# Attention with routed experts: the row maxima 22 slots ahead from the first unit to the last, a unit's shift turned behind step 22

## What is computed

```python
# x: [4, 1024, 128]; 16 heads of 8 dimensions
q, k, v = split(layernorm(layernorm(x)) @ w_qkv + b_qkv)
scores = q @ k.T * 8 ** -0.5 + rel_bias[h, i - j]
attn = softmax(scores) @ v
x = x + layernorm(attn @ w_out + b_out)
# 64 experts: a token takes 8 of them, out of its 4 best groups of 8
topk_idx, topk_w = route(layernorm(x) @ gate.T)
x = x + layernorm(experts(layernorm(x), topk_idx, topk_w) + shared(layernorm(x)))
```

## Time and profile before

| | before |
|---|---|
| median of 3 runs | 1193.54 us (1192.19 to 1193.61) |
| profiled execution, its own time | 1190.53 us |
| its span in the trace | 1188.6 us |
| mean granted TensorE clock | 0.87 of full |
| busy: PE, DVE, ACT, POOL | 883.5, 789.2, 689.8, 592.6 us |
| first step of unit 0, of unit 31 | 113.06 us, 867.30 us |
| PE idle ahead of `turn_shift` (L1328) for POOL | 8.3 us in 12 of 32 |

### The profile page before, as it was taken

How to read it: one execution, slowest core, us unless ns; L and a number is a source line. 1 busy time by engine, 2 the same in 40 slices (tenths; PEclk the granted TensorE clock), 3 DMA queues, 4 the chain that set the end, 5 groups by cost and what they waited for, 6 DMA issues and landing times. The chain is left out here.

```text
span 1188.6 us, 16268 instructions
## 1 busy us (share of the span) xinstructions
PE 883.5 (74%) x5090; PEld 274.5 (23%) x5090; DVE 789.2 (66%) x1222; ACT 689.8 (58%) x1433; POOL 592.6 (50%) x734
## 2 busy tenths in 40 slices
PE   4653999999889999989999998999973530555400
PEld 2410222222222222222222222222211320444300
DVE  7864888889869989968988987998711320111107
ACT  4721767787767777768778776777771210322204
POOL 5820010114255555635745644555575756478747
PEclk9865999999989999999999999999996675655655
DMA  3859523012211122220001120000000010767546
GB/s 99 242 157 133 113 65 103 20 37 65 71 54 27 30 56 73 67 46 7 8 14 36 39 69 15 5 5 16 6 5 22 19 46 3 182 130 135 99 96 208
DMA packets 110379, 77.97 MB, mean 66 GB/s; under 512 B 35359, under 2 KB 95259, under 8 KB 110294
## 3 DMA queue, kind: packets, MB, share of 16 engines
q1 hardware_dynamic: 87062, 68.21, 21.9%
q0 software_dynamic: 21504, 6.79, 4.8%
q10 hardware_dynamic: 1728, 1.94, 1.0%
HBM read 38.75 MB, written 54.95 MB: 79 GB/s over the span
## 5 line engine op out<-in xcount | busy, mean ns | idle before, releaser
L209 DVE TENSOR_REDUCE half_max<-s_pair 128x2 f32<-128x1024 f32 x512 | 601.9, 1217 | 113.1 <-PE s_pair L198 109.5
L1248 ACT ACTIVATE probs<-st_bank 128x512 f32<-128x512 f32 x1024 | 543.8, 603 | 171.6 <-PE st_bank L1308 171.2
L1111 POOL DMA_INDIRECT table<-rows,keys_i x256 | 256.7, 1003 | 179.4 <-issue 68.3
L1308 PE MATMUL st_bank<-q_stack,k_stack 98*128 98x512 bf16 (+1 forms) x1024 | 326.1, 390 | 10.1 <-ACT probs L1248 7.6
L1317 PE MATMUL pv_bank<-probs,values 128*9 128x512 f32 x2048 | 270.4, 600 | 3.1 <-ACT unit_out L1182 3.0
L198 PE MATMUL s_pair<-k_stack,q_stack 64*128 64x512 bf16 x1024 | 204.0, 398 | 41.4 <-DVE half_max L209 22.0
L198 PEld LDWEIGHTS s_pair<-k_stack,q_stack 64*128 64x128 bf16 x1024 | 49.4, 93 | 359.6 <-issue 185.2
L1491 POOL DMA_INDIRECT sums<-out,ids x64 | 99.7, 1558 | 40.7 <-ACT out L1546 18.4
L1308 PEld LDWEIGHTS st_bank<-q_stack,k_stack 98*128 98x128 bf16 (+1 forms) x1024 | 78.2, 97 | 170.1 <-issue 75.8
L1505 DVE CAST ids<-xe 128x4 uint32<-128x4 f32 x16 | 2.9, 180 | 136.2 <-DMA sums<-out,ids 84.5
L1005 POOL CAST shift<-minus_max 128x16 bf16<-128x16 f32 x32 | 6.4, 201 | 111.7 <-DVE minus_max L215 111.6
(11 more groups left out here) (181 smaller groups left out, 788.4 us busy)
## 6 DMA issues: line engine op xcount, KB each, us to landing
table<-blank SPq DMA_DIRECT2D x8, 772.0 KB, 7.4
xe<-table SPq DMA_DIRECT2D x16, 386.0 KB, 4.8
q_stack<-q_image SPq DMA_DIRECT2D x96, 64.0 KB
k_stack<-k_image SPq DMA_DIRECT2D x96, 64.0 KB
s<-sums SPq DMA_DIRECT2D x24, 256.0 KB, 6.0
k_image<-k_piece SPq DMA_DIRECT2D x16, 256.0 KB, 3.3
table<-rows,keys_i POOLq DMA_INDIRECT x256
sums<-zeros SPq DMA_DIRECT2D x16, 256.0 KB
```

The costliest lines, as they stand in the source:

```text
L209: nc.vector.tensor_reduce(halves[:, h:HG:SIDE_HEADS, tile, half], stacks.s_pair[slot % S_SLOTS][:].rearrange("p (s k) -> p s k", s=SIDES), ...
L1111: pool.indirect_dma_start(out=table, out_offset=bass.IndirectOffsetOnAxis(ap=keys_i[c % 2][:, pick:pick + 1], axis=0), in_=rows[c % 2][:, ...
L1248: A.activation(probs[:, s % P_SLOTS, :], st_bank[at % ST_BANKS][:], ACT.Exp).then_inc(bank_free, 1)
L1308: M(bank(at)[:], k_stack[g][own, tile // PER, h, tile % PER * P:(tile % PER + 1) * P], q_stack[g][own, half, h, :], start=True, stop=True) ...
```

## The change

`LEAD` becomes one number, 22. Before, 20 slots were ahead at the first step, and one more was added each 16 steps until 26 were. Now slots 16 to 21 stand ahead of unit 0 (before 16 to 19), and each even step takes one slot, step s the slot s/2 + 22. A unit's last slot, which stood behind step 10 from unit 3 on (step 20 in unit 0, 16 in unit 1, 14 in unit 2), stands ahead of step 18's scores in every unit. The shift is turned behind step 22 in every unit (before 22, 20 and from unit 2 on 18). `SPLIT` goes from place 3 to place 5. The number of instructions of each kind stays as it was.

```diff
-LEAD, FIRST_LEAD = 26, 20
+LEAD = 22
...
-SPLIT, SCATTER = 3, 3 * TILES_T + 4
-def MTURN(n):
-    return (22, 20)[n] if n < 2 else 18
-def issued(step):
-    return min(ALL_UNITS * SLOTS, step // 2 + 1 + FIRST_LEAD + min(LEAD - FIRST_LEAD, step // 16))
+SPLIT, SCATTER = 5, 3 * TILES_T + 4
+J_MTURN = 22
 def slots_at(n, j):
-    step = n * STEPS + j
-    return range(issued(step - 2) if step else FIRST_LEAD, issued(step)) if j % 2 == 0 else ()
+    slot = (n * STEPS + j) // 2 + LEAD
+    return (slot,) if j % 2 == 0 and slot < ALL_UNITS * SLOTS else ()
...
-            for slot in range(SLOTS, FIRST_LEAD):
+            for slot in range(SLOTS, LEAD):
                 row_max(dve, nc, stacks, slot, shift_done)
...
-            for slot in range(SLOTS, FIRST_LEAD):
+            for slot in range(SLOTS, LEAD):
                 row_scores(pe, nc, stacks, slot)
...
-                    if n < ALL_UNITS - 1 and j == MTURN(n):
+                    if n < ALL_UNITS - 1 and j == J_MTURN:
                         turn_shift(n + 1)
```

## The result

The changed kernel took 1216.58 us (median of 4 runs, 1214.32 to 1217.39); the kernel before, with the runs beside them, 1192.87 us. The ratio is 1.0198, with a 95% interval from 1.0179 to 1.0216: 23.7 us slower, where +19.4 was forecast. The profiled execution took 1216.12 us and has a span of 1214.2 us, 25.6 more than before; that is more than the medians' 23.7 because the profiled execution of the kernel before was a short one (1190.53 us).

What follows compares the result with a forecast made beforehand. PE was taken to bound the kernel, DVE second. Start -4.7, six turns +14.4, clock +6.6 and unit 30 +3.1 gave +19.4 us, 1213 us against the runs' median; eight-in-ten range 1203 to 1221 us.

Steps and rivals of the forecast that it cites:

- The stall of the six units: Units 6, 10, 14, 18, 22, 26: split waits behind `group_order`, PE stalls 2.6 us; net 2.4 each, 14.4 in all.
- The clock: Half clock behind about two thirds of the stalls in units 6 to 26, 1.6 us a fall: 6.6 us in all.
- The rival in which the clock holds: The stalls come but the clock stays up: +12.8 us, 1206 us; chance 0.16.
- The start: Unit 0 on: 5.2 us from six second slots and 0.9 at unit 0's turn, less 1.4 at step 0: -4.7 us.
- 22 to 22.5 given as a sign: Sign of being right: units 1 to 3 about 22 to 22.5 us long instead of 23 to 24.3.
- Unit 30: Slots to step 18 and a later turn there, with a stall over 3 us and its clock: 3.1 us late.
- What I costed at nothing: The turns outside units with n % 4 == 2, and the transfers of the shift: 0 us.
- a tail that I took to move along unchanged: From 888 us on, the tail follows from unit 31 and moves with it, with no cost of its own.
- The thin turns: Rival: 20 other turns each 0.3 us or more late, or transfers land late: +26 to +32, about 1221 us; chance 0.14.
- waits at the turn in other units: Sign of being wrong: PE waits at the turn outside units 6, 10, ..., 26 and 30.

Runs made afterwards that it cites:

- run 2: Kernel before with its own growing lead, but the shift turned behind step 22 and split at place 5, behind `group_order`: 1215.26 us, 1.0205 of before.
- run 1: Changed kernel with the split ahead of `group_order` and `residual_norm` at place 5 in every unit: 1194.87 us, 1.0042 of before.
- run 5: Changed kernel with the split ahead of `group_order` in units with n % 4 == 2 alone: 1190.53 us, 0.9995 of before.
- run 8: Changed kernel with the split ahead of `group_order` in units with n % 4 == 2 alone, and the turn behind step 20: 1202.24 us, 1.0091 of before.
- run 7: Kernel before with its growing lead (20 to 26), split at place 5 behind `group_order`, turn behind step 24 in every unit: 1191.86 us, 1.0001 of before.
- run 4: Changed kernel with the split back at place 3, slots and turn as changed: 1226.34 us, 1.0306 of before.
- run 3: Changed kernel with the turn behind step 24 in place of 22, all else as changed: 1184.55 us, 0.9959 of before.
- run 6: Changed kernel with the split ahead of `group_order` in units with n % 4 == 2 alone, and the turn behind step 24: 1185.03 us, 0.9954 of before.

## Why the prediction was right

**The stall of the six units, as forecast.** The chain `group_sums`, `group_order`, split, turn was read off before, and each link came within 0.2 us. Forecast were 2.6 us of wait and 2.4 net; the trace has 2.57 us in all six (units 14 and 22 show 2.89, where a score's 0.32 us has no record), and by run 2's units without a fall the net is 2.1. Runs 1 and 5 show the cause: the same slots and the same turn with the split ahead of `group_order` leave +0.1 us.

**The clock, a term too small.** Forecast were falls behind two thirds of the stalls at 1.6 us, 6.6 us. It fell behind all six, at 1.5 us: 9 us. The two terms together were 21.0 forecast and 21.5 measured, the one over and the other under, so that their sum comes so near is partly luck. In run 2 the clock fell behind four of six equal stalls, the two thirds of the forecast; that it fell behind all six here is one execution's count. The rival in which the clock holds would have needed what units 14 and 22 of run 2 did in all six. The Trainium skill (page "TensorE: Matmul & The Clock Gate", section "Why this matters for your kernels") asks that idle gaps between bursts of matmuls stay under some three microseconds. In these runs that isn't enough: 1.46 us in run 8 and 2.35 us in run 2 were followed by half clock.

**The start, right with luck.** Forecast -4.7, measured +0.7 - 5.4 = -4.7. But the forecast was 6.1 us gained in units 0 to 3 and 1.4 lost at step 0; both came 0.7 us smaller, and the errors cancel. A second slot costs less than 0.86 us: the units lost 5.4 us, of which the wait at unit 0's turn was 0.9, so 4.5 us for six slots, some 0.75 each. (Unit 2, at 22.82 us, is above the 22 to 22.5 given as a sign.) Step 0 came later by 0.7 us here and by 0.7 to 1.8 in the other runs with six slots ahead of it (113.76 us and not 114.5). Run 7 confirms the size of the flat lead's gain.

**Unit 30.** +3.1 forecast, +3.9 measured. The turn came where it should, 18.0 us behind the unit's first exponential as in the six others; behind a stall of 3.53 us the half clock lasted twice as long as before, a loss of 3.4 us of full speed instead of 1.7.

**What I costed at nothing.** The trace is 25.6 us longer and the forecast was 19.4; of the 6.2 us between them 4.9 are in places that I put at nothing. The turns of the other units: 2.1 us together, most of it in units 15 and 23 (+0.6 each). PE waited 0.56 us there for an exponential. ACT had started it late, and so had DVE its slot, at the same moment, here in unit 15:

```profile
497.74 0.39 PE L198 MATMUL s_pair<-k_stack,q_stack 64*128 64x512 bf16 x2
498.06 0.60 PE L1302 MATMUL st_bank<-q_stack,k_stack 98*128 98x512 bf16 x2
...
499.10 2.36 DVE L209 TENSOR_REDUCE half_max<-s_pair 128x2 f32<-128x1024 f32 x2 [0.76 <-PE s_pair L198]
499.13 1.58 ACT L1242 ACTIVATE probs<-st_bank 128x512 f32<-128x512 f32 x3 [1.27 <-PE st_bank L1302]
```

So what was late is what both wait for, PE's matmuls or the signal that they are done, and not ACT; why stays open. The wait for the attention rows in units 16 and 24: PE stood 3.51 us in unit 16, as before (3.59 in the earlier trace rows), but the half clock behind it lasted twice as long. The windows row of the changed kernel (answers to the earlier trace rows):

```profile
525.00:545.00 20.00, 15.70 (x75) 4.34 (x74) 11.35 (x18) 10.77 (x23) 7.12 (x10) 0.83 0.07 13
```

20 x 0.17 = 3.4 us of full speed lost, 1.7 before. The two units are 2.9 us longer, and that was in no term. In unit 8 the same wait was shorter (4.70 us, before 5.54), which gave 1.0 back. Run 4, with the slots and the turn of the changed kernel, had the shorter half clock in both units behind the same waits, so slots and turn don't force the longer one; what decides isn't shown. The last 0.9 us are behind unit 31's first exponential, a tail that I took to move along unchanged; they weren't looked into.

**The thin turns.** The rival that put 0.3 us or more on twenty turns didn't come. Of the other turns only those of units 15 and 23 had a wait that long, which is the sign "waits at the turn in other units" in two places, and it wasn't POOL that ended it. (Unit 5 shows 0.40 us for POOL; 0.32 of it is a score without a record.) The margin was as thin as stated: in units 9, 17, 25 and 29 PE waited 0 to 0.1 us. Runs 1 and 4 show another thin place: `residual_norm` at (1, 5) ended 2.5 and 5.4 us later in unit 17 than in the changed kernel, and ACT stood 1.27 and 4.18 us for it.

## What to carry to other kernels

When an engine's order is written out, a short piece that others wait for must not stand behind one that waits for a late event of the same stretch. Look at each kind of stretch: the same place in the order healed the units with `group_order` and hurt those with `residual_norm`. A stall in a matmul-bound stretch can have a second price in the clock, here 1.5 us on 2.1 where it fell. And the slack between a result and its consumer is cheap to buy by moving the consumer: two steps later made the changed kernel 0.4% faster than before instead of 2% slower. The 0.4% itself is the flat lead's (run 7 without it is at 1.0001).

## What was not expected of the hardware

Stalls of the same length were followed by half clock or not, and for two different times. Run 2 had 2.35 us in six units: none in two of them, a loss of 1.7 us of full speed in three, 3.4 in one. Run 4 had 3.2 us in six: 1.7 in three, 3.4 in three. Stalls up to 1.4 us (unit 30 of run 3, 1.39 us) left the clock at 2.4 GHz in the attention of all these traces; 1.46 us (run 8), 1.85 us (unit 30 before) and all the longer ones but the two of run 2 were followed by 1.2 GHz. Behind the waits of units 16 and 24, 3.2 to 4.1 us long, the loss was 1.7 us of full speed in the kernel before and in run 4, 3.4 us in the changed kernel and runs 1, 2, 3, 5 and 8, and one of each in runs 6 and 7. The length of the wait doesn't sort them: 3.48 us lost 1.7 in run 4, and 3.50 us lost 3.4 in run 1. Since each trace is one execution, a difference of 1.5 us between two kernels in one unit may be this and nothing of the change.
